# Flamingo block on one core: context chunks rounded on ScalarE, input norm two batches ahead, hidden layer a step earlier

## What is computed

```python
q, k, v = layernorm(x) @ Wq.T + bq, ctx @ Wk.T + bk, ctx @ Wv.T + bv
s = where(mask > 0.5, clip(q @ k.T / 4, -50, 50), -1e4).clip(-50, 50)   # per head
d = (softmax(s) @ v) @ Wo.T + bo
x = x + tanh(g_xattn) * (layernorm(rs * d) * gamma + beta)
h = silu(bitlinear(layernorm(x), w1)) * bitlinear(layernorm(x), w2)     # 704 wide
x = x + tanh(g_ffn) * bitlinear(h, w3)      # bitlinear: int8 rows, ternary weights
```

## Time and profile before

| | us |
|---|---|
| median of 3 runs (1438.78 to 1439.39) | 1438.97 |
| the profiled execution, its own time | 1438.62 |
| span of the profiled execution | 1436.8 |
| PE busy | 1348.5 (94%) |
| DVE busy | 1131.2 (79%) |
| ACT busy | 965.1 (67%) |
| mean granted clock of PE, of full speed | 0.974 |

### The profile page before, as it was taken

How to read it: one execution, slowest core, us unless ns; L and a number is a source line. 1 busy time by engine, 2 the same in 40 slices (tenths; PEclk the granted TensorE clock), 3 DMA queues, 4 the chain that set the end, 5 groups by cost and what they waited for, 6 DMA issues and landing times.

```text
span 1436.8 us, 48034 instructions
## 1 busy us (share of the span) xinstructions
PE 1348.5 (94%) x19984; PEld 1220.3 (85%) x19984; DVE 1131.2 (79%) x2241; ACT 965.1 (67%) x1634; POOL 469.7 (33%) x759
## 2 busy tenths in 40 slices
PE   5699999999999999999999999999999999999982
PEld 5599888888988888898888898888889888888971
DVE  6668788878878887877887887888788788878763
ACT  2367776676776767777676777767777767676751
POOL 3523333233333223233323333332333332232310
PEclk9699999999999999999999999999999999999995
DMA  7467666666766666776667676666667666766620
GB/s 217 110 160 174 157 153 156 164 158 167 169 163 155 154 163 166 168 169 156 156 152 171 161 176 160 158 150 161 163 162 173 158 157 155 167 163 162 139 52 8
DMA packets 142477, 222.13 MB, mean 155 GB/s; under 512 B 29162, under 2 KB 135598, under 8 KB 142254
## 3 DMA queue, kind: packets, MB, share of 16 engines
q1 hardware_dynamic: 129966, 199.31, 57.7%
q0 software_dynamic: 12288, 19.69, 6.2%
HBM read 54.00 MB, written 3.28 MB: 40 GB/s over the span
## 4 chain that ended last, share of the span: by engine, by line
PE 52%; DVE 25%; ACT 13%; issue 7%; POOL 2%; SPq 1%; DMA 0%; DVEq 0%; POOLq 0%; ACTq 0%
PE pvb L1212 13%; PE sc L1192 12%; PE cb L1233 11%; PE cb L1247 9%; ACT e_sb L549 7%; DVE e_sb L783 4%; DVE zt L855 3%; DVE c_lo L750 2%; PE mb L1280 2%; PE mb L1271 2%; DVE tiny L935 2%; PE mb L1298 2%; DVE k_lo L774 2%; DVE th L945 1%; ACT us L623 1%
## 5 line engine op out<-in xcount | busy, mean ns | idle before, releaser
L549 ACT ACTIVATE e_sb<-sc 121x800 f32<-121x800 f32 (+1 forms) x768 | 644.8, 844 | 201.4 <-PE sc L1192 191.3
L1192 PE MATMUL sc<-q_st,k_st 96*121 96x200 f32 (+1 forms) x3072 | 476.4, 278 | 7.1 <-DMA q_st<-bd_hi 3.1
L1192 PEld LDWEIGHTS sc<-q_st,k_st 96*121 96x121 f32 (+1 forms) x3072 | 416.3, 186 | 42.5 <-issue 9.0
L783 DVE TENSOR_SCALAR e_sb<-e_sb,hi_b 121x1600 f32<-121x1600 f32 (+1 forms) x384 | 399.4, 1047 | 38.3 <-ACT e_sb L549 38.1
L1212 PE MATMUL pvb<-e_sb,v_sb 121*32 121x100 f32 x12288 | 286.2, 251 | 0.1
L1212 PEld LDWEIGHTS pvb<-e_sb,v_sb 121*32 121x32 f32 x12288 | 264.7, 110 | 22.6 <-issue 19.0
L774 DVE SCALAR_TENSOR_TENSOR k_lo<-cb,bk_c,k_hi 128x484 fp32r<-128x484 f32 (+1 forms) x192 | 134.4, 700 | 137.8 <-ACT k_hi L561 137.8
L1247 PE MATMUL cb<-wv_hi,c_hi 128*121 128x256 f32 (+1 forms) x768 | 227.8, 297 | 15.2 <-DVE k_lo L774 12.2
L475 POOL DMA_DIRECT2D q_st<-bd_hi x256 | 183.2, 719 | 107.9 <-DVE bd_lo L829 104.7
L1247 PE MATMUL cb<-wv_hi,c_lo 128*121 128x256 f32 (+1 forms) x768 | 217.0, 283 | 0.0
L1247 PE MATMUL cb<-wv_lo,c_hi 128*121 128x256 f32 (+1 forms) x768 | 216.9, 282 | 0.0
(11 more groups left out here) (139 smaller groups left out, 1609.0 us busy)
## 6 DMA issues: line engine op xcount, KB each, us to landing
k_st<-k_hi SPq DMA_DIRECT2D x512, 121.0 KB, 2.8
c_in<-in_ctxT SPq DMA_DIRECT2D x64, 484.0 KB, 3.8
k_st<-k_lo SPq DMA_DIRECT2D x256, 121.0 KB, 2.9
k_st<-k_hi SPq DMA_DIRECT2D x256, 119.0 KB, 2.3
c_in<-in_ctxT SPq DMA_DIRECT2D x32, 476.0 KB, 3.6
k_st<-k_lo SPq DMA_DIRECT2D x128, 119.0 KB, 2.4
q_st<-bd_hi POOLq DMA_DIRECT2D x256, 50.0 KB, 3.3
q_st<-bd_lo POOLq DMA_DIRECT2D x128, 50.0 KB, 3.2
```

The costliest lines, as they stand in the source:

```text
L549: nc.scalar.activation(e_sb[e_slot(b, n)][0:TL[n], k * SW:(k + 1) * SW].rearrange("p (o c) -> p o c", o=2), sc[q % NSC][0:TL[n], :, 0:2 * PW],
L783: V.tensor_scalar(e, e, E_LO, hi_b[b.par][0:TL[n], n:n + 1], ALU.max, ALU.min).then_inc(clip_done, 1)
L1192: last = T_.matmul(sc[q % NSC][0:TL[n], e // 2, (e % 2) * PW:(e % 2 + 1) * PW], k_st[st_slot(b, n // TPC)][:, pr // NQ, pr % NQ, t0:t0 + T ...
```

## The change

- The cast `c_hi` leaves DVE in the normal pass: ACT makes it (`chunk_head`) in steps 1, 5, 9, between the two exponentials. `split_rest` moves to steps 2, 6, 10, at the end of the step's first half. One semaphore for both becomes two.
- The input norm is done for the batch after the next: `x_stats` and `x_aggr` in step 9, the root on POOL after `residual` in step 11, `x_norm` in step 11.
- The gates and up-projections come earlier (PE: g0 in step 8, u0 and g1 in 9, u1 in 10), DVE's `hidden_gate` and `hidden_up` in steps 9 and 10, `h_max` in 11. `result` comes before the clip of step 2.
- `hq` and `hT` are padded from 704 to 768 columns (zeros), so that the last tile is a full one and ACT copies `hT` in one instruction.

```diff
-        hq = sb("hq", [S, F], bf16)
+        hq = sb("hq", [S, FT * P], bf16)
 # SP: every wait on split_done "lo{u}" becomes
+                    sp.wait_ge(c_lo_done, CHUNK.after(b.plus(1), 0))
 # POOL batch
-                            x_rstd_of(b.plus(1))
                             mask_of(b.plus(1))
...
                     if n == 11 and nxt:
                         residual(b.plus(1), prev)
+                        if nxt2:
+                            x_rstd_of(b.plus(2))
 # ACT
+            def chunk_head(b, u):
+                slot, n = c_slot(b, u)
+                w = CL[u]
+                pu, pb = (u - 2) % NCH, (b if u == 2 else b.plus(-1))
+                act.wait_ge(c_loaded[slot], 16 * (n + 1))
+                act.wait_ge(pe_ctx, CTX.after(pb, f"v{pu}1"))
+                nc.scalar.activation(c_hi[slot][:, :, 0:w], c_in[slot][:, :, 0:w], ACT.Copy).then_inc(c_hi_done, 1)
...
                     exps(b, n, 0)
+                    if nxt and n % 4 == 1 and not b.base:
+                        chunk_head(c, n // 4)
...
                     if prev and n in (9, 10):
-                        ffn_gate(d, n - 9)
-                    if prev and n in (9, 11):
-                        ffn_up(d, (n - 9) // 2)
+                        ffn_up(d, n - 9)
+                    if prev and n in (8, 9):
+                        ffn_gate(d, n - 8)
                     exps(b, n, 1)
 # DVE batch
-                    if nxt and n % 4 == 1:
+                    if b.base and nxt and n % 4 == 1:
                         split_head(c, n // 4)
...
-                        if n == 3:
-                            x_aggr(c)
-                        if n == 6:
-                            q_head(c)
-                    if prev2 and n == 0:
-                        hidden_gate(b.plus(-2), 1)
+                    if nxt and n == 6:
+                        q_head(c)
                     if prev:
                         if n == 2:
                             attention_out(d)
-                        if n == 10:
-                            hidden_gate(d, 0)
+                        if n in (9, 10):
+                            hidden_gate(d, n - 9)
+                    if nxt2 and n == 11:
+                        x_norm(b.plus(2))
+                    if prev2 and n == 2:
+                        result(b.plus(-2))
                     if n:
                         clip(b, n - 1)
...
-                    if nxt and n % 4 == 1:
+                    if nxt and n in (2, 6, 10):
                         split_rest(c, n // 4)
                     if prev2 and n == 0:
-                        hidden_up(b.plus(-2), 1)
-                        for step in (h_max, h_scale, h_round, h_quant):
+                        for step in (h_scale, h_round, h_quant):
                             step(b.plus(-2))
-                    if prev2 and n == 2:
-                        result(b.plus(-2))
-                    if nxt and n == 2:
-                        x_stats(c)
-                    if nxt and n == 3:
-                        x_norm(c)
+                    if nxt2 and n == 9:
+                        x_stats(b.plus(2))
+                        x_aggr(b.plus(2))
...
-                        if n == 10:
-                            hidden_up(d, 0)
+                        if n in (9, 10):
+                            hidden_up(d, n - 9)
+                        if n == 11:
+                            h_max(d)
 # PE: down and h_turn without the short last tile
-                    m = P if k < FT - 1 else FL
-                    last = T_.matmul(mb[0:S, 0:H], hT[0:m, k, :], w3q[0:m, k, :], start=k == 0, stop=k == FT - 1)
+                    last = T_.matmul(mb[0:S, 0:H], hT[:, k, :], w3q[:, k, :], start=k == 0, stop=k == FT - 1)
...
+                        if n == 8:
+                            up(d, 0, 0)
                         if n in (9, 10):
-                            up(d, n - 9, 0)
-                        if n == 11:
-                            up(d, 1, 1)
+                            up(d, n - 9, 1)
                     attend()
...
                     if prev and n == 9:
-                        up(d, 0, 1)
+                        up(d, 1, 0)
```

More of the change, by code:

```diff
@@ L353, in batch @@
                 if nxt2:
-                    sp.wait_ge(split_done, SPLIT.after(b.plus(1), "lo1"))
+                    sp.wait_ge(c_lo_done, CHUNK.after(b.plus(1), 1))
                     load_c(b.plus(2), 0)
@@ L358, in batch @@
                 if nxt2:
-                    sp.wait_ge(split_done, SPLIT.after(b.plus(1), "lo2"))
+                    sp.wait_ge(c_lo_done, CHUNK.after(b.plus(1), 2))
                     load_c(b.plus(2), 1)
@@ L478, in stack_q, with batch @@
                         ).then_inc(q_stacked[b.par], 16)
-            def batch(b, nxt, prev):
+            def batch(b, nxt, prev, nxt2=True):
                 for n in range(NT):
@@ L521, in passes @@
                 residual(whole(0, base), False)
+                x_rstd_of(whole(1, base))
                 batch(whole(0, base), True, False)
                 if base:
-                    with pool.Fori(base // 2, (base + NB - 2) // 2) as i:
+                    with pool.Fori(base // 2, (base + NB - 4) // 2) as i:
                         batch(Batch(2 * i + 1, i, 1, base), True, True)
                         batch(Batch(2 * i + 2, i + 1, 0, base), True, True)
+                    batch(whole(NB - 3, base), True, True)
                 else:
-                    for n in range(1, NB - 1):
+                    for n in range(1, NB - 2):
                         batch(whole(n), True, True)
-                batch(whole(NB - 1, base), False, True)
+                batch(whole(NB - 2, base), True, True, False)
+                batch(whole(NB - 1, base), False, True, False)
                 delta_rstd(whole(NB - 1, base))
@@ L743, in split_head @@
                             guard(c_in[slot][:, k, p.start:min(p.stop, w)], care_c, GUARD_C, b, f"{u}{k}{i}")
-                V.tensor_copy(c_hi[slot][:, :, 0:w], c_in[slot][:, :, 0:w]).then_inc(split_done, 1)
+                V.tensor_copy(c_hi[slot][:, :, 0:w], c_in[slot][:, :, 0:w]).then_inc(c_hi_done, 1)
             def split_rest(b, u):
@@ L965, in result, with batch @@
                     y.then_inc(result_done, 1)
-            def batch(b, nxt, prev, prev2):
+            def batch(b, nxt, prev, prev2, nxt2=True):
                 own = prev
@@ L1123, in passes @@
                         v_guard(b, u, 1)
+                x_stats(whole(1, base))
+                x_aggr(whole(1, base))
+                x_norm(whole(1, base))
                 batch(whole(0, base), True, False, False)
@@ L1127, in passes @@
                 if base:
-                    with dve.Fori(base // 2 + 1, (base + NB - 2) // 2) as i:
+                    with dve.Fori(base // 2 + 1, (base + NB - 4) // 2) as i:
                         batch(Batch(2 * i + 1, i, 1, base), True, True, True)
                         batch(Batch(2 * i + 2, i + 1, 0, base), True, True, True)
+                    batch(whole(NB - 3, base), True, True, True)
                 else:
-                    for n in range(3, NB - 1):
+                    for n in range(3, NB - 2):
                         batch(whole(n), True, True, True)
+                batch(whole(NB - 2, base), True, True, True, False)
                 e = whole(NB - 1, base)
-                batch(e, False, True, True)
+                batch(e, False, True, True, False)
                 clip(e, NT - 1)
-                hidden_gate(e.plus(-1), 1)
-                hidden_up(e.plus(-1), 1)
-                for step in (h_max, h_scale, h_round, h_quant, result):
+                for step in (h_scale, h_round, h_quant, result):
                     step(e.plus(-1))
@@ L1224, in k_item @@
                     if o == 0:
-                        pe.wait_ge(split_done, SPLIT.after(b, f"lo{u}"))
+                        pe.wait_ge(c_lo_done, CHUNK.after(b, u))
                     if not (isinstance(b.n, int) and b.n == 0 and u == 0):
```

31 lines of the change are left out of this document (14 added, 17 removed).

## The result

Four runs of the changed kernel gave a median of 1376.84 us (1375.27 to 1382.12), four of the kernel before beside them 1439.18 (1438.78 to 1439.76). The ratio is 0.9573, with an interval of 0.9547 to 0.9599: 62 us faster, where 48 were forecast and 1384 was the low end of the range. The profiled executions stand 62.4 apart (1438.62 and 1376.26), so the traces can account for the difference of the medians.

A forecast was written before the change was run, and what follows sets the result against it. PE sets the pace, losing time waiting for DVE. Per batch 1.29 + 0.20 + 0.18 - 0.10 = 1.57 us; 29 batches give 45.5, ends 2.7; 1438.6 - 48.2 = 1390.4, stated as 1390 us, range 1384 to 1412.

The forecast's parts named there:

- Hidden lateness of DVE, 1.29 a batch: PE's waits for DVE from step 0's scores to `delta`, 0.92 of it before `delta`; all 1.29 us per batch goes.
- `hT` padded to full tiles: At `down`'s sixth weight load, a 0.18 us idle gap goes; gain 0.18 per batch, between 0 and 0.3.
- Step 7, 0.20: PE's second `k_lo` wait of a batch, in step 7, goes: 0.20 us per batch.
- Ends, 2.7: First and last batches: last batch wins 2.3 us, batch 1 wins 0.9, batch 0 loses 0.5; 2.7 in sum.
- Leftover for late keys, 0.10: At step 0, stacked keys land about 0.5 us later, leaving 0.1 us per batch of PE waiting; bounds 0 to 1.0.
- Rival one: Chunk load ahead of `k_st` on SP makes stacked keys 1.1 us late each batch: 1419 us; chance 0.19.
- rival two: On SP, late `c_lo` of chunk 1 delays load and `k_st` copies, keys 2.6 us late: 1466 us; chance 0.07.
- What moving `c_lo` is for: On DVE before `attention_read`, moving `c_lo` behind `result` takes out 1.07 us of the 3.6 removed.
- 3.6 us taken out where DVE was 1.5 late: DVE's steps 0 to 3 lose 3.6 us before `attention_read`, which was 1.5 late, so it then waits for PE.
- Input norm at cost 0: Statistics in step 9, root and norm in step 11: DVE saves a wait of about 0.8 us; cost 0.
- The copies on ACT: Each 968-column copy in steps 1, 5, 9 takes 0.98 us, covered by ACT's idle time there.
- Spare of 1.1: DVE's `result` ends at 734.3, PE reaches `delta` at 735.5; about 1.1 us spare.

The follow-up runs named there:

- first run: Changed kernel with short tiles again in the transposes of the hidden row, the ACT copy and `down`: 1397.04 us, ratio 0.9709 to the kernel before.
- The last two runs: Changed kernel with the `k_st` copies ahead of the chunk load in SP's order: 1372.55 us; changed kernel with `c_lo` back at steps 1, 5, 9: 1368.72 us.

## Why the direction was right and the size wrong

- *Hidden lateness of DVE, 1.29 a batch.* Right: 1.37 by the table, `delta` never waits in a middle batch. Taking the last batch as a control gave this size to within 0.1.
- *`hT` padded to full tiles.* **This step failed**, as a term mis-sized: "Gain 0.18, at most 0.3 with the way back to full rows". It measured 0.54 (first run), 0.31 for `down` and 0.23 for the transposes. Two errors. I priced the idle gap ahead of the short weight load and gave the way back no price of its own; measured, the way in costs 0.09 and the way back 0.21. The Trainium skill (TensorEngine Tiling (Array Packing), Key Properties) says that a change of the tiling mode drains the engine; a short last tile would be two such changes, which is the larger figure of the prediction, and the trace agrees in that both sides cost and add up to 0.3. No run shows that a drain is the reason. And I looked for a gap only where the trace prints one: the transposes' sixth tile is 64 columns wide in its weights, shows none, and yet costs 0.23. With 0.54 for 0.18, 29 x 0.36 = 10.4 us, the forecast would have been 1380; of the other 4 us, the two stretches with waits gave 0.16 a batch more than the sum had (4.6 us), batch 1 gave 2.2 more, and the waits left over took 0.13 a batch more (3.8 us).
- *Step 7, 0.20.* 0.28. I counted the `k_lo` wait and not that the transposes behind it also came 0.09 sooner.
- *Ends, 2.7.* Batch 1 won 3.1 where I had 0.9; no run says why. The last interval won 1.8 and what follows it 0.5, together the 2.3 that I had. In batch 0 the first `delta` came 0.4 later, for 0.5 forecast.
- *Leftover for late keys, 0.10.* All that stands above the shortest period grew by 0.23, but less than half of it is keys: PE's weight loads wait for them in 5 of 27 batches, 2.4 us or 0.09 a batch (3 batches and 1.2 us before). Two waits put down to "issue" (1.5 us) are the largest part of the rest. Rival one's wait is thus there, by rival two's mechanism: SP's first copy follows `c_lo` and not the scores. I held that DVE would be 3.5 us earlier at that point and so ruled it out; `c_lo` ended 0.3 after the scores instead of before. The last two runs, which put the order right in two ways, are some 4 and 8 us faster. (Rival two's 1466 leaves out the 2.7 of the ends; with them it is 1463.)
- *What moving `c_lo` is for.* I made it a part of the gain (1.07 of the 3.6 taken out ahead of `attention_read`). With it back in its old steps `delta` still never waits. It was not needed, and it costs. The rows say why: the move took one `c_lo` out of DVE's stretch ahead of `attention_read`, from step 1 to 2, and put another into it, from step 9 to 10.
- *3.6 us taken out where DVE was 1.5 late.* That should have left some 2 us of idle time before `attention_read`; the median is 0.09. DVE reaches it 1.6 us sooner (1.48 of lateness gone, 0.09 idle) and not 3.6. The step held, but barely. By the rows, `c_lo` and most of the hidden layer's 1.9 were moved within the stretch and not out of it.
- *Input norm at cost 0.* Wrong as a reason, right in the sum: it took nothing, but without it the new order loses 49 us. I priced the part against the old order of DVE, in which the transposes of x hardly ever waited, and not against the order that the other parts leave.
- *The copies on ACT.* 1.026 us for 0.98, covered, as said. Taking the move back costs 4.7 us (with the uncertainty said above), although nothing of the shortest period.
- *Spare of 1.1.* From `attention_read` to the end of `result` it took 706.39 - 701.74 = 4.65, for 4.63 forecast. But the padding lies on PE's way to `delta`, and the 0.36 by which it gave more came off the spare: 1.1 - 0.36 = 0.7. Of that, 0.15 is the time from the end of DVE's instruction to the start of PE's.

Open: why the waits above the shortest period grow when PE's period does (the three runs with short tiles); two waits of PE of up to 0.9 us that the trace puts down to "issue"; half of what moving `c_lo` back brings; and how the price of the old norm divides between the clip and `c_lo`.

## What to carry to other kernels

A stage that waits for one engine's chain gains by a cut of that chain only up to the spare; price each part of a change by undoing it alone in the *new* order, as parts with no price of their own (the norm) can carry most of the gain and named parts (`c_lo` moved) can cost. In an in-order queue, ask for each entry whether what it waits for ends before what the entries behind it wait for. And for a tile of odd size, take the distance from the group's start to the next group's, and compare with a group of full tiles: the idle gap that the trace prints is not the cost.

## What the runs showed of the hardware

- One 64-wide tile at the end of a group of six cost PE 0.31 us in the matmuls (64 rows) and 0.23 in the bf16 transposes (64 columns of weights), though it is half the work of a full one: 0.09 ahead of it in both, the rest behind it.
- Two waits of 0.7 and 0.8 us within 3 us, PE busy 1.53 of the 3, were followed by a fall of the granted clock from 2.4 to 1.2 GHz for about 3.4 us in 4 batches of the kernel before with the padding, and by none in its other batches. In the kernel with the old place of the norm, one wait of 1.4 us per batch was followed by none.
- The median landing time of a `k_st` copy was 2.6 us before and 3.8 us after, where the chunk load is issued right in front of the copies. With `c_lo` back in its old steps it was 2.7. The DMA engines' mean busy share from 200 to 1260 us was 0.68, 0.72 and 0.70, so the share alone does not account for it.
